# A new order for the first stage of a two-stage kernel: units split in quarters, a third halving in the column sums, early rows for the router

## The reference

```
x = x + tanh(g_xattn[0]) * matmul(q(layernorm(x)), q(ctx))          # q: round to 0..255, clip, take off the zero point, scale
x = x + tanh(g_ffn[0])   * ( h @ base_W.T + 2 * top-2-of-8 LoRA (rank 16) of h )   # h = layernorm(x)
```

## Time and profile before

| | |
|---|---|
| time, median of 3 runs | 1067.0 us (1066.91 to 1068.57) |
| time of the profiled execution | 1069.01 us |
| its span, first to last instruction | 1067.3 us |
| PE busy | 1022.5 us, 96% of the span |
| DVE, ACT, POOL busy | 75%, 45%, 20% |
| mean granted TensorE clock | 0.997 of full speed |

### The profile page before, as it was taken

How to read it: one execution, slowest core, us unless ns; L and a number is a source line. 1 busy time by engine, 2 the same in 40 slices (tenths; PEclk the granted TensorE clock), 3 DMA queues, 4 the chain that set the end, 5 groups by cost and what they waited for, 6 DMA issues and landing times.

```text
span 1067.3 us, 13150 instructions
## 1 busy us (share of the span) xinstructions
PE 1022.5 (96%) x5047; PEld 771.0 (72%) x5072; DVE 799.2 (75%) x1106; ACT 482.9 (45%) x502; POOL 217.0 (20%) x123
## 2 busy tenths in 40 slices
PE   0899999989999999999999999999999999999998
PEld 0344444444698888888887878898788889888887
DVE  7789799979568754757788678968867897855554
ACT  6873585530243232233444445644443555433432
POOL 2254547599505242400000000000000000000000
PEclk9999999999999999999999999999999999999999
DMA  9793698838488878653776876758588586668765
GB/s 371 270 367 146 269 351 314 305 133 303 163 322 329 304 273 304 230 185 102 225 295 196 281 263 191 273 184 312 186 272 281 178 280 184 197 201 306 241 199 178
DMA packets 85198, 265.89 MB, mean 249 GB/s; under 512 B 7312, under 2 KB 15504, under 8 KB 77456
## 3 DMA queue, kind: packets, MB, share of 16 engines
q1 hardware_dynamic: 67472, 231.50, 61.9%
q10 hardware_dynamic: 17664, 33.56, 8.5%
HBM read 214.70 MB, written 50.33 MB: 248 GB/s over the span
## 4 chain that ended last, share of the span: by engine, by line
PE 70%; DVE 18%; DMA 5%; ACT 4%; issue 3%; SPq 0%; ACTq 0%; DVEq 0%
PE acc L1394 15%; PE acc L1396 15%; PE acc L1395 15%; PE acc L1372 14%; DVE w_lo L1118 4%; PE aT_psum L1464 2%; DMA w_stage<-w_sums_scratch 2%; DVE S_sum L1214 1%; PE aT_psum L1443 1%; PE aT_psum L1442 1%; ACT ctx_u L755 1%; DMA w_stage<-in_wt 1%; DVE S_lo L1222 1%; DVE c_acc L1192 1%; DVE ctx_pair_sums L1037 1%
## 5 line engine op out<-in xcount | busy, mean ns | idle before, releaser
L1118 DVE TENSOR_TENSOR w_lo<-w_stage,w_hi 128x1024 fp32r<-128x1024 f32 x200 | 249.3, 1258 | 160.0 <-ACT w_hi L815 159.5
L815 ACT ACTIVATE w_hi<-w_stage 128x1024 fp32r<-128x1024 f32 x200 | 209.5, 1058 | 333.7 <-PE acc L1396 258.4
L1394 PE MATMUL acc<-w_hi,S_hi 128*128 128x512 f32 x384 | 151.4, 394 | 2.0 <-DVE w_lo L1118 1.6
L1396 PE MATMUL acc<-w_hi,S_lo 128*128 128x512 f32 x384 | 149.7, 390 | 0.0
L1395 PE MATMUL acc<-w_lo,S_hi 128*128 128x512 f32 x384 | 149.5, 389 | 0.0
L1372 PE MATMUL acc<-ctx_quant,aT_even 128*128 128x512 bf16 x500 | 115.1, 387 | 5.1 <-ACT aT_even L763 4.1
L1394 PE MATMUL acc<-w_hi,A_hi 128*128 128x512 f32 x288 | 114.0, 396 | 0.3
L1396 PE MATMUL acc<-w_hi,A_lo 128*128 128x512 f32 x288 | 112.4, 390 | 0.0
L1395 PE MATMUL acc<-w_lo,A_hi 128*128 128x512 f32 x288 | 112.2, 390 | 0.0
L1372 PE MATMUL acc<-ctx_quant,aT_odd 128*128 128x512 bf16 x499 | 111.5, 379 | 0.7
L695 POOL TENSOR_TENSOR t_job<-t_job 128x1024 f32<-128x1024 f32 x32 | 84.3, 2636 | 107.8 <-DMA t_job<-in_wt 106.6
(11 more groups left out here) (180 smaller groups left out, 1630.2 us busy)
## 6 DMA issues: line engine op xcount, KB each, us to landing
w_stage<-in_wt SPq DMA_DIRECT2D x104, 512.0 KB, 4.6
w_stage<-w_sums_scratch SPq DMA_DIRECT2D x96, 512.0 KB, 4.3
ctx_stage<-in_ctx SPq DMA_DIRECT2D x32, 1024.0 KB, 7.6
t_job<-in_wt SPq DMA_DIRECT2D x8, 2048.0 KB, 10.4
w_sums_scratch<-t_job SPq DMA_DIRECT2D x8, 2048.0 KB, 9.5
c_acc<-x_scratch SPq DMA_DIRECT2D x32, 512.0 KB, 5.9
out<-c_acc ACTq DMA_DIRECT2D x64, 256.0 KB, 5.4
x_rows<-x_scratch SPq DMA_DIRECT2D x11, 1024.0 KB, 8.1
```

What stands on the lines that cost most here:

```text
L815: ins = act.activation(wh[i % HI][:, :], raw[:, :], ACT.Copy)
L1118: ins = dve.tensor_tensor(low[:, :], raw[:, :], high[:, :].bitcast(F32), ALU.subtract)
L1394: pe.matmul(out_, lh, rh, start=first, stop=False, skip_group_check=onto)
L1396: return pe.matmul(out_, ll, rh, start=False, stop=final, skip_group_check=onto)
```

## The change

1. `SPLIT_UNITS`: units 0 to 31 (all of the first batch) are issued on PE in four quarters of 4 matmuls, each of which waits for one piece of the block (`c_conv`) and not for all four. The quarters 0 to 2 have numbers of their own (`QUARTER_SLOT`), so that quarters of up to four units stand between one another; the last quarter stands at the unit's number.
2. All tables are new: the order of loads, of the units, and of every step on every engine.
3. `ctx_sums` halves a third time (4 slices to 2, 128x1024), and `col_sums` has 2 matmuls in place of 4.
4. `x_scale` has five tiny operations in place of six.
5. Two copies of transposed tiles (8 and 9) go from ACT to DVE (`COPY_ACT`); `WIDEN_ACT` has 11 tiles in place of 9.
6. The first two `transpose_h` stand ahead of the last unit on PE, and three `w_lo` and two `h_lo` stand ahead of the last `evac` on DVE.

```diff
-LOAD_ORDER = 'xxccxcccxccccccxccccxcccxxxxcccxccxcccxccccxccxx'
+LOAD_ORDER = 'xccxcxccccxcccccxcccxccxcxxxxxccccccccccxxccxcxc'
-WIDEN_ACT = [1, 2, 3, 4, 5, 8, 11, 14, 15]
+WIDEN_ACT = [0, 2, 3, 4, 5, 6, 7, 8, 11, 12, 13]
+COPY_ACT = [0, 1, 2, 3, 4, 5, 6, 7, 10, 11, 12, 13, 14, 15]
+EARLY_H = 2
...
             def x_scale(t):
 
                 dve.wait_ge(std_ready, t + 1)
-                rstd(link, xve[:, t:t + 1], xsd[:, t:t + 1], xrs[:, :])
-                link(dve.tensor_scalar(qs[:, t, 0:1], xrs[:, :], inv1, None, ALU.mult))
+                v, y, n = xve[:, t:t + 1], xrs[:, :], nt[:, 0:1]
+                link(dve.reciprocal(y, xsd[:, t:t + 1]))
+                link(dve.scalar_tensor_tensor(out=n, in0=y, scalar=y, in1=v, op0=ALU.mult, op1=ALU.mult))
+                link(dve.tensor_scalar(n, n, -0.5, 1.5, ALU.mult, ALU.add))
+                link(dve.scalar_tensor_tensor(out=qs[:, t, 0:1], in0=y, scalar=inv1, in1=n, op0=ALU.mult, op1=ALU.mult))
...
                 dve.tensor_tensor(pair[:, 0:K // 4, :], pair[:, 0:K // 4, :], pair[:, K // 4:K // 2, :], ALU.add)\
+                    .then_inc(sums_halved, 1)
+                dve.wait_ge(sums_halved, c + 1)
+                dve.tensor_tensor(pair[:, 0:K // 8, :], pair[:, 0:K // 8, :], pair[:, K // 8:K // 4, :], ALU.add)\
                     .then_inc(sums_ready, 1)
...
+            def aT_copy(t):
+                g, m = t // M, t % M
+                dve.wait_ge(tp_ready, t + 1)
+                if g >= 2:
+                    dve.wait_ge(pe_unit, last_of_tile(t - 2 * M) + 1)
+                dve.tensor_copy(aT[g % 2][:, :, m * P:(m + 1) * P], tpa[:, :, :]).then_inc(aT_by_dve, 1)
...
                 if s in EVAC_AT:
+                    if EVAC_AT[s] == M * ITS - 1:
+                        for i in range(HI - 1):
+                            w_lo(i)
+                        for k in range(EARLY_H):
+                            h_lo(k)
                     evac(EVAC_AT[s])
...
-            def unit(p):
+            def unit(p, q0=0, q1=CP):
+
                 t, c = UNITS[p]
                 g, m = t // M, t % M
-                pe.wait_ge(c_conv, CP * (c + 1))
-                wait_aT(pe, t)
-                if p >= M:
-                    pe.wait_ge(bank_read, p - M + 1)
-                for k in range(K):
+                pe.wait_ge(c_conv, CP * c + q1)
+                if q0 == 0:
+                    wait_aT(pe, t)
+                    if p >= M:
+                        pe.wait_ge(bank_read, p - M + 1)
+                for k in range(PK * q0, PK * q1):
...
-                for k in range(K // 4):
-                    ins = pe.matmul(colp[:, :], ones[:, :], pair[:, k, :], start=(k == 0), stop=(k == K // 4 - 1))
+                for k in range(K // 8):
+                    ins = pe.matmul(colp[:, :], ones[:, :], pair[:, k, :], start=(k == 0), stop=(k == K // 8 - 1))
...
+                    if UNIT_AT[s] == M * ITS - 1:
+                        for k in range(EARLY_H):
+                            transpose_h(k)
+                    p = UNIT_AT[s]
+                    unit(p, CP - 1 if p in SPLIT_UNITS else 0)
+                if s in QUARTER_AT:
+                    p, q = QUARTER_AT[s]
+                    unit(p, q, q + 1)
```

More of the change, by code:

```diff
@@ L115 @@
                   COPY_SLOT, STORE_SLOT, JOB_SLOT, GROUP_STATS_SLOT, NORMALISE_SLOT))
+QUARTER_AT = {slot: (SPLIT_UNITS[i // 3], i % 3) for i, slot in enumerate(QUARTER_SLOT)}
 LAST_STORE = STORE_SLOT.index(max(STORE_SLOT))
@@ L118 @@
 PLACE = {unit: p for p, unit in enumerate(UNITS)}
+EARLY_H = 2
+assert UNIT_BLOCK[-1] in (NB + 1, NB + 3)
 HK = K // 2
@@ L391, in build @@
         tp_ready = sem("tp_ready")
-        aT_ready = sem("aT_ready")
-        aT_moved = [sem(f"aT_moved{s}") for s in range(2)]
+        aT_by_act = sem("aT_by_act")
+        aT_by_dve = sem("aT_by_dve")
         xr_ready = sem("xr_ready")
@@ L450, in wait_widened, with wait_aT @@
                 eng.wait_ge(a_by_dve, sum(w <= t and w not in WIDEN_ACT for w in range(TILES)))
-        def wait_transposed(eng, t):
-            if t < PE_TILES:
-                eng.wait_ge(tp_ready, t + 1)
-            else:
-                eng.wait_ge(aT_moved[t % 2], 16 * sum(w % 2 == t % 2 for w in range(PE_TILES, t + 1)))
-        def wait_aT(eng, t):
-            if t < PE_TILES:
-                eng.wait_ge(aT_ready, t + 1)
-            else:
-                eng.wait_ge(aT_moved[t % 2], 16 * sum(w % 2 == t % 2 for w in range(PE_TILES, t + 1)))
+        def wait_aT(eng, t):
+            if t in COPY_ACT:
+                eng.wait_ge(aT_by_act, sum(c <= t for c in COPY_ACT))
+            else:
+                eng.wait_ge(aT_by_dve, sum(c <= t and c not in COPY_ACT for c in range(TILES)))
         def half(t, h):
@@ L1076, in normalise, with w_lo, h_lo @@
                     chain(ins)
+            def w_lo(i):
+                g, kind, s, pc = PIECES[i]
+                dve.wait_ge(wh_ready, i + 1)
+                raw, low, high = wst[i % RAW], wl[i % RAW], wh[i % HI]
+                if kind == "AR":
+                    both = arv[i % HI]
+                    ins = dve.tensor_tensor(both[:, :, 1, :], raw[:, 0:WK * AR].rearrange("p (k n) -> p k n", n=AR),
+                                            both[:, :, 0, :].bitcast(F32), ALU.subtract)
+                elif kind == "L":
+                    ins = dve.tensor_tensor(low[:, 0:NW], raw[:, 0:NW], high[:, 0:NW].bitcast(F32), ALU.subtract)
+                else:
+                    ins = dve.tensor_tensor(low[:, :], raw[:, :], high[:, :].bitcast(F32), ALU.subtract)
+                ins.then_inc(wl_by_dve, 1)
+            def h_lo(k):
+                dve.wait_ge(hh_ready, k + 1)
+                dve.tensor_tensor(hl[:, k, :], th0[k % 3][:, :], hh[:, k, :].bitcast(F32), ALU.subtract)\
+                    .then_inc(hl_ready, 1)
             for s in range(SLOTS):
+                if s in COPY_AT and COPY_AT[s] not in COPY_ACT:
+                    aT_copy(COPY_AT[s])
                 if s in CWIDEN_AT:
@@ L1223, in combo_rest @@
                     .then_inc(combo_lo, 1)
-            for i in range(HI - 1):
-                w_lo(i)
             for k in range(K):
-                h_lo(k)
+                if k >= EARLY_H:
+                    h_lo(k)
                 if k % 2 == 1:
@@ L1466, in fill @@
                 ins.then_inc(fill_done, 1)
-            for k in range(3):
+            for s in range(SLOTS):
+                if s in UNIT_AT:
+                    if UNIT_AT[s] == M * ITS - 1:
[6 more added lines that the diff above has]
+                    unit(p, q, q + 1)
+                if s in COLMM_AT:
+                    col_sums(COLMM_AT[s])
+                if s in MOVE_AT:
+                    transpose_a(MOVE_AT[s])
+            for k in range(EARLY_H, 3):
                 transpose_h(k)
```

139 lines of the change are left out of this document (53 added, 86 removed), and 4 rows, old and new, of the table QUARTER_SLOT.

## The result

The changed kernel takes 1073.1 us in the median of 12 executions (1069.8 to 1078.2), before took 1068.2 beside it (12 executions); the ratio is 1.0048 with a 95% interval of 1.0035 to 1.0061. It is slower by 0.5%, where 1.4% faster was forecast.

A forecast was written before the change was run, and what follows sets the result against it. PE was taken as the bound, busy 1022.5 of 1067.3 us. Gains of 6.4 + 1.5 + 3.5 + 2.3 + 1.7 = 15.4 us gave a forecast of 1051.6 us, range 1047 to 1059.

The forecast's parts named there:

- The opening: Start of stage one: quarters and new order let PE start earlier, losing 27.3 us against 33.7; gain 6.4 us.
- the vanished clock dip: Granted clock of 0.63 at 44 to 48 us, after a 4.09 us idle time, goes; gain 1.5 us.
- The column sums: Stage one: two of four matmuls go, 0.44 us in each of eight blocks on PE; gain 3.5 us.
- The bound of 1.2 us: Upper bound for one third halving (128x1024) on DVE, expected at 0.7 us; 6.5 us taken for eight.
- DVE's account as a whole: DVE over stage one: halvings +6.5, copies +4.6, widenings -4.6, scales -2.6; sum +3.9 us.
- The end of stage one: Handover to the router: PE's 2.31 us idle time goes (2.3 us), and the low clock behind it (1.7 us).
- Later waits: Stage one after the opening: 4.1 us lost there (5.6 less 1.5) stay, as one wait or another.
- three signs of being wrong: PE waits for ctx_quant or x_group over 5 us (60-260 us); DVE above 95% (60-200); clock under 1.00 after 45 us.
- a chain that the prediction had named for the opening alone: Rival, chance 0.09: ACT waits for DVE's scales, tile 2's copy stays at 44 us, opening not earlier; 1058.0 us.
- Stage two is the same program and not touched: Stage two, after the router starts: assumed unchanged, so no term was counted for it.
- The slower rival of the prediction: Opening and first batch: quarters' many short waits keep the clock low, 17.5 us lost; 1069.1 us, chance 0.06.
- The rival of DVE and POOL in one another's way: First batch: POOL's column terms hold up DVE's adds, 8 us more on DVE, 5 reaching PE; 1056.6 us, chance 0.25.

The follow-up runs named there:

- the jobs apart: Changed kernel, third job's store moved among the W pieces, POOL's second-job steps earlier, third-job steps behind stage one's other work: 1060.8 us, 0.9918 of before.
- store_last: Changed kernel with the third job's 2 MB store issued behind weight pieces 6 and 7 instead of ahead: 1069.4 us, 0.9987 of before.
- jobs_early: Changed kernel, third job's store behind pieces 6 and 7, POOL's second- and third-job steps at earlier slots: 1070.4 us, 1.0001 of before.
- before_jobs_late: Kernel before, with POOL's second- and third-job steps moved to their later places in the changed kernel: 1075.4 us, ratio 1.0050.

## Why the prediction was wrong

**The opening** (6.4 us): right. Lost there were 39.86 less 11.7 us of work, 28.2, against 33.7: 5.5 us. The first quarter (24.15), PE without a break (39.86) and the vanished clock dip (1.00 from 44 to 48) came as they were named.

**The column sums** (3.5 us): what each takes off PE, 0.44 us, is right, the term is not. On before the halving costs 5.7 us, in the new order leaving it away changes nothing. The prediction put 0.7 us on one halving, 1.2 at most, and 6.5 on the eight; the group of DVE in after, over 20 to 280 us, says 1.30 in the mean and 10.4 in all, with the copies from PSUM behind it. The last two rows, over 0 to 286 us, are the widening of the context, in before and in after:

```profile
L1044 DVE TENSOR_TENSOR ctx_pair_sums<-ctx_pair_sums 128x1024 f16<-128x1024 f16 x8 | 10.4, 1301 | 0.3
...
L1019 DVE COPY aT_even<-aT_psum 128x2048 bf16<-128x2048 bf16 x2 | 2.4, 1215 | 0.0
...
L1029 DVE TENSOR_SCALAR ctx_quant<-ctx_u 128x2048 bf16<-128x2048 uint16 x32 | 35.4, 1133 | 1.9 <-ACT ctx_u L755 1.9
...
L1030 DVE TENSOR_SCALAR ctx_quant<-ctx_u 128x2048 bf16<-128x2048 uint16 x32 | 24.1, 767 | 12.1 <-ACT ctx_u L758 12.1
```

The halving is held up by POOL like the longer sums. The bound of 1.2 us scaled the hold-up with the length of what is held up; the rows show that it lasts as long as POOL's instruction still runs (2.34 us at 171.78), however short the halving is. I had read DVE as busy 90.31 of 92 us, and still counted as a gain what takes 0.44 us off PE and puts 1.30 on DVE. DVE's account as a whole came near its estimate, +2.8 us by the two page heads against +3.9, by luck: the halvings cost 10.4 and not 6.5, the two copies 2.4 and not 4.6, and the scales, with a step fewer, saved nothing (37.6 us, before 36.7); against that the context's widening took 11.3 us less, which the prediction did not have.

**The end of stage one** (2.3 + 1.7 us): right as a mechanism. The router started at once. The early rows alone are worth 4 us on before.

**Later waits** ("the 4.1 us lost there stay"): 6.4 us of waits for rows, 0.5 for a copy, and (1 - 0.92) x 20 = 1.6 of low clock in 220 to 240, together 8.5. By the sum the last unit was to end at 281.43 - 6.4 - 1.5 - 3.5 = 270.0; it ended near 277.6. Of these 7.6 us, 4.4 are the later waits (8.5 in place of 4.1), 0.9 the opening, and 1.1 the two transpositions of rows that now stand ahead of the last unit; 1.2 stay open. Of the prediction's three signs of being wrong, only the clock under 1.00 appeared: DVE was busy 88% from 60 to 200 us (and 97% from 180 to 280, where the sign did not look), and PE did not wait for `ctx_quant` or a bank, but for rows, by way of DVE's scale and ACT, a chain that the prediction had named for the opening alone. Ahead of the longest of these waits (2.39 us at 220.27) the last step of a scale runs beside two job steps (timelines of DVE and of POOL):

```profile
212.26 2.29 DVE L1004 SCALAR_TENSOR_TENSOR quant_scale_bias<-x_mean_var,quant_scale_bias,scalars 128x1 f32<-128x1 f32 x1
...
212.19 4.79 POOL L700 TENSOR_TENSOR t_job<-t_job 128x1024 f32<-128x1024 f32 x2
```

The same step takes 0.22 us at 219.56. So the jobs had a hand in this loss too, as far as one profile tells; no run moved these steps.

**The step that failed** is the sentence "Stage two is the same program and not touched". It is the same program, but its first weights stand in SP's queue behind the stores of jobs 1 and 2, and those behind eight steps of POOL, whose table the change moved. The prediction counted 64 column terms on POOL and not the jobs. It let the time at which the first router matmul begins stand for the time at which the router stage ends: it put the change of the router stage at -1.7 us, the low clock, and it was +10.8 (34.8 against 24.0). What it cost is shown from both sides: the table alone makes before 0.5% slower, the table and the store put right make after 1.3% faster, 0.8% of it by the store's place (0.9972 against 1.0048), 0.5% by the steps' (0.9918 against 0.9972). The slower rival of the prediction (a clock held low by quarters) did not happen; the clock fell behind waits of 2.39 and 3.71 us, at 220 us and in the router stage. The rival of DVE and POOL in one another's way was at work, though not as it was priced: in the third halvings, and in the scales and the router's subtractions beside job steps, where it had not looked.

With the jobs apart the change is worth 0.8%, 8.8 us, or 10.2 by the first W matmul, of 15.4 forecast; of the missing 5.2, 0.9 are the opening, and the rest PE lost again in waits behind it. Since the kernel is as fast without the third halving, 3.5 of the 5.2 can be put on the column sums. Open is why stage two after the first W matmul differs between kernels whose code is nearly the same there: 758.1 us to the end in before, 757.1 in store_last, 760.1 with the jobs apart, 763.7 in after. In after's profile PE waits there longer for `w_lo` and `x_rows` (3.1 and 2.6 us, in before 1.6 and 1.1), but its execution was the slowest of twelve, and no run was made for it.

## What to carry to other kernels

When an order is rewritten, follow every queue past the end of the stretch that is rewritten: list for each engine and for the queue of transfers what is issued last in it, who waits for that first, and when. An early start is worth nothing if what is needed next comes at the old time or later. Before taking work from the bounding engine by giving some to another, look at that one's windows: here DVE was busy 98% of one, and 0.44 us less on PE for 1.30 us more on DVE brought nothing in one order and a loss in the other. And price a small instruction beside a helper engine by the helper's instruction, not by its own length.

## What the runs showed of the hardware

**A DVE subtraction of two operands in SBUF takes from 2.21 to 6.18 us for the same three instructions, by what POOL does meanwhile.** With one column term of POOL beside them they take 2.21 (jobs_apart), with two job steps 5.59 (jobs_early), and with a job step, a column term and a job step one after another 6.18 (before_jobs_late); there each subtraction seems to wait for the end of one instruction of POOL. The next instruction, the low half of the rows with one operand in PSUM, took 0.68 us beside a job step. The Trainium skill (SBUF - State Buffer, "Who interferes with whom") states this: a vector instruction with two SBUF inputs and a GpSimd instruction that reads SBUF exclude each other for the whole instruction, while one with at most one SBUF input, outside the two-port modes, does not contend. These runs agree. What it comes to for a small instruction is several times its own length: the single subtraction took 0.44 and 2.09 us in after, the step of a scale on one element a row 0.22 and 2.29.

**A copy of 128x2048 bf16 from PSUM on DVE took 1.22 us**, the mean of the two in the rows above. The prediction had taken 2.28 from a row of another kind, and set beside it an estimated 1.2 by the Trainium skill (VectorE: DVE Perf Modes, "Why PSUM operands drop a tier"); the measurement is with the page.

**Each wait of 3.71 us in the router stage of after** stands ahead of a stretch of lower granted clock: 0.57 in the 4 us from 288.00, and 0.50, the lower of its two levels (1.2 and 2.4 GHz), in the 3.7 us from 299.28. The wait of 2.39 us at 220.27 is followed by 0.58 over 3.7 us; the waits of 1.2 and 1.0 us at 104 and 115 us left the clock of their window (100 to 120 us) at 1.00. In the router stage the clock took 4.8 us, beside the waits' 7.7.
